# Feed-forward activations of layer 1 quantised inside the attention, its gate and up weights put in place there

## The reference

```python
x = x + _L1_xattn_ref(_layernorm(x), ctx, Wq_d, W_qk, Wkv_d, Wv_u)      # 16 heads, latent keys and values
x = x + _L1_ffn_ref(_layernorm(x), w_gate, w_up, w_down, s_gate, s_up, s_down)

def _L1_ffn_ref(x, ...):            # H = 512, I = 1376
    xq = int4_quant(x)              # beta = mean |x| of the row; clip(round(x * sqrt7 / (beta + eps)), -8, 7)
    gate = bitlinear(xq, w_gate, s_gate)     # w_q = clip(round(w / (mean |w| + eps)), -1, 1), times mean |w|
    up = bitlinear(xq, w_up, s_up)
    inter = int8_quant(up * square(relu(gate)))   # gamma = max |.| of the row; round(x * 127 / gamma)
    return bitlinear(inter, w_down, s_down)
```

## Time and profile before

| | us |
|---|---|
| median of 3 runs | 850.58 (850.53 to 852.6) |
| the profiled execution | 852.77 |
| its span | 851.1 |
| attention of layer 1, last unit's copy ends | 177.02 |
| its last VectorE operation ends | 181.09 |
| first gate matmul | 188.85 |
| last down matmul of the feed-forward part ends | 229.61 |
| first operation of layer 2 | 230.0 |

### The profile page before, as it was taken

One profiled execution on the slowest core, in us unless ns is written; L12 is line 12 of the kernel. 1 busy time (PEld: TensorE's weight loads), 2 busy tenths in 40 slices (PEclk: granted clock), 3 DMA queues, 4 the chain that ended last, 5 costly groups with the idle time before them and its releaser, 6 DMA issues. The chain is left out here.

```text
span 851.1 us, 16359 instructions
## 1 busy us (share of the span) xinstructions
PE 778.3 (91%) x5144; PEld 634.7 (75%) x5150; DVE 700.9 (82%) x1762; ACT 532.3 (63%) x1441; POOL 408.9 (48%) x374
## 2 busy tenths in 40 slices
PE   1995899858988999999999999999999999899988
PEld 0484666534677898898888988989989888776556
DVE  7897988969787887897897897798888888797855
ACT  6865798846457557557657657665665576772541
POOL 3237088805035845844846746745755663401120
PEclk9998999979999999999999999999999999999879
DMA  8245246444120310320320320320310210004001
GB/s 299 108 144 180 77 151 240 145 133 142 29 72 21 106 50 1 99 74 0 99 74 0 99 74 0 99 73 1 99 49 25 75 50 26 1 2 120 1 1 50
DMA packets 37488, 65.67 MB, mean 77 GB/s; under 512 B 5377, under 2 KB 17729, under 8 KB 37314
## 3 DMA queue, kind: packets, MB, share of 16 engines
q1 hardware_dynamic: 37442, 65.10, 23.3%
HBM read 59.76 MB, written 5.33 MB: 76 GB/s over the span
## 5 line engine op out<-in xcount | busy, mean ns | idle before, releaser
L2433 DVE TENSOR_SCALAR_CACHE_REDUCE xn<-ctxT,candidate 128x512 bf16<-128x512 f32 x240 | 168.8, 741 | 0.0
L2080 ACT ACTIVATE layer_attention_probs<-xnT,stats 128x512 f32<-128x512 f32 x128 | 94.0, 734 | 119.2 <-DVE stats L2222 119.2
L1818 PE MATMUL bank<-layer_attention_keysT,layer_attention_queriesT 128*128 128x512 f32 x384 | 120.5, 422 | 5.1 <-DVE layer_attention_queriesT L2215 5.0
L2234 DVE TENSOR_TENSOR layer_attention_probsT<-bank,layer_attention_probsT 128x512 fp32r<-128x512 f32 x128 | 88.1, 688 | 41.2 <-ACT layer_attention_probsT L2088 39.8
L1818 PEld LDWEIGHTS bank<-layer_attention_probsT,layer_attention_values 128*128 128x128 f32 x768 | 98.2, 188 | 11.9 <-DVE layer_attention_probsT L2234 4.2
L2088 ACT CAST layer_attention_probsT<-bank 128x512 fp32r<-128x512 f32 x128 | 74.8, 585 | 50.5 <-PE bank L1901 50.4
L1818 PE MATMUL bank<-layer_attention_probsT,layer_attention_values 128*128 128x256 f32 x768 | 101.5, 281 | 3.3 <-DVE layer_attention_probsT L2234 2.7
L1818 PE MATMUL bank<-layer_attention_l_wkv,layer_context_parts 128*128 128x256 f32 x720 | 93.7, 283 | 0.0
L1818 PE MATMUL bank<-layer_attention_l_wq,layer_attention_xnT 128*128 128x512 f32 x384 | 93.6, 392 | 0.0
L1818 PEld LDWEIGHTS bank<-layer_attention_l_wkv,layer_context_parts 128*128 128x128 f32 x720 | 91.3, 191 | 2.7
L1818 PE MATMUL bank<-layer_attention_wo,layer_attention_headsT 128*128 128x512 f32 x336 | 88.7, 405 | 0.4 <-ACT layer_attention_squares L2039 0.4
(11 more groups left out here) (347 smaller groups left out, 1673.2 us busy)
## 6 DMA issues: line engine op xcount, KB each, us to landing
layer_attention_l_raw_qo<-in_wqT SPq DMA_DIRECT2D x8, 1024.0 KB, 5.5
layer_attention_l_raw_qo<-in_woT SPq DMA_DIRECT2D x8, 1024.0 KB, 6.4
xnT<-inverse_sums SPq DMA_DIRECT2D x14, 512.0 KB, 3.8
tw_raw<-in_w_gateT SPq DMA_DIRECT2D x8, 688.0 KB, 5.2
tw_raw<-in_w_upT SPq DMA_DIRECT2D x8, 688.0 KB, 4.2
tw_raw<-in_w_downT SPq DMA_DIRECT2D x6, 768.0 KB, 4.6
layer_attention_l_raw_kv<-in_wkvT SPq DMA_DIRECT2D x8, 512.0 KB, 5.0
ternary<-tw_rounded SPq DMA_DIRECT2D x8, 344.0 KB, 2.5
```

Of the source, the lines that this page charges most:

```text
L1818: last = pe.matmul(out, stationary[f][a], moving[f][b], start=f == 0 and x == 0, stop=f == count - 1 and x == 2)
L2080: a.activation(probs[:, u % 3, :], masked[:, u % 2, :], ACT.Exp, bias=negmax[:, u:u + 1], scale=-1.0, accum_out=sums[:, u:u + 1]).then_inc ...
L2234: v.tensor_tensor(probsT[:, 1, p % 2, :, columns], T[u % 2][:, :].rearrange("p (c q) -> p c q", c=CPB), probsT[:, 0, p % 2, :, columns], A ...
L2433: own(k.nc.vector.tensor_scalar((k.flags if flags is None else flags)[:, r % 2], row_tile(k.ctxT, r), k.candidate[:, r:r + 1].bitcast(F32) ...
```

## The change

Tiles 0 and 1 are quantised and turned at the end of the attention block instead of at the start of the feed-forward block. Their codes, the up weights and half of the turned codes lie where batch 0's queries were, the gate weights in `xnT` and, with the passes of the quantising, where batch 0's values were. The pieces are rounded in the order gate, down, up; up pieces are written in place and not stored, gate weights are loaded back behind pieces 10, 11 and 12. The feed-forward block starts with the matmuls; the last tile's attention result is added to `x` there, and tiles 2 and 3 are quantised between the first tile's chunks. The update of the bisection moves from u = 55 to u = 62, two counts from the start to the end of the feed-forward block. The chunk after a tile's row maximum comes ahead of its scaling. GpSimd's splits wait for the 8-bit codes of tiles 0 and 1.

```diff
+    ROUNDED = (0, 1, 2, 3, 8, 9, 10, 11, 12, 4, 5, 6, 7)
+    STORED = 9
...
+        if i == tw.STORED:
+            g.wait_ge(scores_psum, TPB * HEADS1)
+        rounded = tw.rounded[0:rows, n % 2, 0:width] if i < tw.STORED else k.front.up[:, f, :]
...
+    for i, piece in enumerate(tw.ROUNDED):
+        if 2 <= i < tw.STORED + 2:
             store(i - 2)
+        elif i >= 2:
+            sp.wait_ge(tw.rounded_ready, i - 1)
+        ternary_load(k, piece, count + i)
+        if i == tw.STORED + 1:
+            for p in range(2):
+                sp.wait_ge(tw.stored[p], 16 * (KT // 2))
+            sp.wait_ge(latent_psum, B)
+            gate_load(0, k.front.gate[0])
+        if i == tw.STORED + 2:
+            gate_load(1, k.front.gate[1])
+        if i == tw.STORED + 3:
+            sp.wait_ge(quads_done, TPB * HEADS1 // 4)
+            gate_load(2, k.front.gate[2])
...
+def front_magnitudes_scalar(k, n, t):
...
+    a.activation(r.x4[:, t, :], k.xn[:, t, :], ACT.Abs, accum_out=r.beta[:, t:t + 1]).then_inc(r.beta_ready, 1)
...
                 turn_mixed(TILES - 1)
+                for t in range(TPB):
+                    front_turn_tensor(k, t)
...
+                    if u == UNITS - 1:
+                        v.wait_ge(S_["probs_ready"], UNITS)
+                        own(v.reciprocal(k.front.inverse[:, :], sums[:, TILES - 1, :]))
                     if u % 4 == 3:
                         copy_turned(u)
...
-                        if counts == 4:
-                            bisection_update(k, own)
+                    if u == UNITS - 2:
+                        bisection_update(k, own)
...
-                divide_mixed(TILES - 1)
-                add_mixed(TILES - 1)
-                v.wait_ge(S_["x_updated"], TILES)
+                front_rounded_vector(k, own, 0)
+                front_codes_vector(k, own, 0)
+                v.wait_ge(S_["mixed_psum"], TILES)
+                v.wait_ge(S_["x_updated"], TILES - 1)
...
+                    if u == 60:
+                        front_magnitudes_scalar(k, following, 0)
...
+                front_magnitudes_scalar(k, following, 1)
+                front_magnitudes_scalar(k, following, 2)
                 copy_mixed(TILES - 1)
...
-                for c, (c0, c1) in enumerate(CHUNKS):
-                    for w in (GATE, UP):
-                        sp.dma_start(wgu[:, w, :, c0:c1], tw.scratch[w].rearrange("(f p) c -> p f c", p=P)[:, :, c0:c1])\
...
+                        if i == 1:
+                            front_magnitudes_scalar(k, n, TILES - 1)
+                        if (t, c) == (2, 0):
+                            x8T_copy(0)
+                    if t == 1:
                         x4T_copy(2)
                         x4T_copy(3)
-                    if t >= 1:
+                    if t >= 2:
                         x8T_copy(t - 1)
...
-                quantise4(0)
-                tile_rows_vector(k, n, TILES - 1)
-                quantise4(1)
...
-                bisection_count(k, own, 0, first_flags(k))
-                for c in range(NC):
-                    inner_chunk(0, c)
-                    if c == 0:
-                        bisection_count(k, own, 1, first_flags(k))
+                scales(0)
+                attention_update()
+                tile_variance_vector(k, TILES - 1)
+                inner_chunk(0, 0)
+                tile_rows_vector(k, n, TILES - 1)
+                inner_chunk(0, 1)
+                front_rounded_vector(k, own, 1)
+                inner_chunk(0, 2)
+                front_codes_vector(k, own, 1)
+                scales(1)
                 for t in range(TILES):
                     magnitude(t)
+                    if t + 1 < TILES:
+                        inner_chunk(t + 1, 0)
                     scaled(t)
                     if t + 1 < TILES:
-                        inner_chunk(t + 1, 0)
+                        inner_chunk(t + 1, 1)
                     own.wait()
                     rounded(t)
-                    if t + 1 < TILES:
-                        inner_chunk(t + 1, 1)
...
                     tile_rows_vector(k, following, t)
+                for j in range(FRONT_COUNTS):
+                    bisection_count(k, own, j, first_flags(k))
...
+                    if t == 0:
+                        pe.wait_ge(x4T_ready, TILES)
...
-                gate_up(0)
-                turn4(2)
-                turn4(3)
-                gate_up(1)
+                pe.wait_ge(tw.gate_loaded, 16 * NC)
+                pe.wait_ge(tw.rounded_ready, len(tw.PIECES))
+                gate_up(0, range(NC))
+                gate_up(1, range(NC))
+                for t in range(TPB, TILES):
+                    pe.wait_ge(x4T_ready, t - 1)
+                    front_turn_tensor(k, t)
+                gate_up(2, range(1))
                 turn8(0)
-                gate_up(2)
+                gate_up(2, range(1, NC))
                 down(0)
                 turn8(1)
-                gate_up(3)
+                gate_up(3, range(NC))
...
+    g.wait_ge(codes_ready, 1)
     g.wait_ge(gw.kv_loaded, 16)
...
+    g.wait_ge(codes_ready, 2)
     g.wait_ge(gw.q_loaded, 16)
```

205 lines of the change are left out of this document (114 added, 91 removed).

## The result

The changed kernel takes 844.41 us in the median (841.79 to 850.39, 10 runs), beside 851.89 of the kernel before (848.17 to 854.68, 10 runs), 7.5 us less. The ratio on record is 0.9927, 95% interval 0.9908 to 0.9947: 6.2 us off (interval 4.5 to 7.8, being 0.0073, 0.0053 and 0.0092 of 851.89). The quotient of the two medians is 0.9912; 0.9927 is what 844.41 gives over 850.58, the median of the first three runs, from which the forecast was made: 7.2 us off, 843.4. The profiled execution of the changed kernel took 842.14 us, its span is 840.4.

A forecast was written before the change was run, and what follows sets the result against it. TensorE, busy 91% of the span, was taken to bound the kernel, with gains only where it waits, chiefly for VectorE's chain. 1.3 + 6.5 - 0.6 = 7.2 us off 850.58 gives 843.4 us, range 841.0 to 848.0.

The forecast's parts named there:

- the stretch: From VectorE's last attention copy to its first layer 2 operation; forecast gain 6.5 us, less 0.6 for the clock.
- Update and magnitudes: Late attention units: moving the update to u = 62 gains 1.3 us; three magnitude passes on ScalarE cost nil.
- Rounding: GpSimd's reordered rounding ends at 169.0 instead of 168.14, tile 0's `rstd` at 169.6; 1.3 us in hand, cost nil.
- Start of the block: Feed-forward start: TensorE begins at about 181.9 instead of 188.85, tile 0's row maximum at 191.0 instead of 197.13.
- Clock: First gate matmuls: a possible fall to half clock after TensorE's short pause, priced at 0.6 us lost.
- Rival A: Clock stays at half through the first two feed-forward chunks: gain 5.6 us, 845.0 us; chance 0.18.
- Tail: Feed-forward end: last norm plus two counts let VectorE end at 223.1, 0.5 us behind TensorE; 6.5 us gained.
- GpSimd's splits: Key, value and query weight splits beside VectorE's scaling and rounding in the feed-forward block: cost nil.
- rival B: Splits block VectorE's scaling or rounding for up to a split operation: gain 5.2 us, 845.4 us; chance 0.14.
- Rival D: Slower: each microsecond of rounding after 170.3 costs one; ending after 180 gives 853.5 us; chance 0.03.
- Rival C: Gate loads slow the piece loads, rounding ends up to 6 us late: 848.1 us at worst; chance 0.10.
- E: The feed-forward block's start is tied to something else, such as the down weights: 850.6 us; chance 0.03.

The follow-up runs named there:

- chunk_first: The kernel before with one edit: the next tile's first chunk product ahead of the scaling. Ratio to the kernel before 1.0023 (0.9995 to 1.0051).
- update_only: The kernel before with only the bisection's update moved, to u = 62 in place of u = 55. Ratio to the kernel before 0.9987 (0.9967 to 1.0006).
- rounding_later: The changed kernel with three more GpSimd passes over the last up piece's raw weights. Ratio to the kernel before 1.0007 (0.9977 to 1.0036).
- splits_free: The changed kernel without GpSimd's two waits for the 8-bit codes ahead of its splits. Ratio to the kernel before 0.9981 (0.9947 to 1.0015).
- before_busy: The kernel before with 18 useless matmuls ahead of the codes' first transposes and 8 ahead of the first gate matmul. Ratio 1.0022 (0.9991 to 1.0053).
- gate_late_busy: The changed kernel with gate transfers only at the feed-forward block's start and 20 useless matmuls in TensorE's wait. Ratio to the kernel before 0.9977 (0.9950 to 1.0004).

## Why the prediction was right, step by step

**The sum.** 1.3 for the update and 5.9 for the stretch (6.5 less 0.6). The traces give 1.86 and 6.06, 7.9 in all; the medians of ten runs 7.5 and the ratio 6.2, with 7.2 inside its interval. The mechanism held in the main, an early front whose two halves are both needed. Part of the close number is luck, as the terms show.

**Update and magnitudes.** The 1.86 us are three terms, not one. The update's move by itself is 1.26 us (chunk_first's 11.51 less update_only's 10.25), as the sum had it. The execution traced of the kernel before adds 1.09 (12.60 less 11.51), most of it with the clock's fall at 170, which the sum didn't have. The magnitudes, put at nil since "the first falls into a wait of ScalarE", cost 0.49. The last two are errors of opposite sign, and the 1.09 aren't there in every execution.

**Rounding.** It ended at 167.39. This execution was 1.42 us ahead already at unit 55 (163.00 against 164.42), so that is 168.8 beside the expected 169.0. The first of GpSimd's three `rstd`, tile 0's, was there at 167.9, 0.55 us behind the rounding, and the norm at 169.38 found it. The margin was 1.5 us (1.3 expected), and rounding_later shows what lay behind it.

**Start of the block.** Counted from the last copy, which the prediction put at 177.2: first gate matmul 4.6 to 4.8 us behind it (expected 4.7), row maximum of tile 0 13.5 (expected 13.8), of tile 3 36.3 (expected 35.8). These terms held.

**Clock.** The 0.6 us were not spent: full clock throughout. TensorE's last down matmul ended 45.1 us behind the copy, and without the 0.6 the prediction had 45.4. I priced the clock only as a small loss of the change, but more hangs on it: with TensorE idle for 4.57 us ahead of the gate matmuls the same block loses 2.15 us more than the lateness. Rival A did not come about there. Further on, behind the idle 2.17 us before the third chunk of tile 1, the clock falls in some executions, and costs 1.1 to 1.2 us, less than A's 1.6. So the trace's 6.06 us for the stretch are those of an execution without that fall.

**Tail.** Predicted 0.5 us of VectorE behind TensorE, measured 1.22. Counted from the copy, TensorE ended 0.3 us sooner than expected and VectorE 0.5 later (46.4 against 45.9). What made VectorE late: the scaling (1.34) and rounding (1.28) of tile 2 lie beside the queries' split and take 0.41 us each over their 0.93 and 0.87.

**GpSimd's splits.** Nil, but for those 0.8 us, is right for the kernel as written and wrong as a view of the machine. The prediction said of rival B that the rows "show less than a third of that". They showed little because few operations met. splits_free shows operations that wait for a whole instruction of GpSimd, one for each small one on 128x2 numbers. The two waits for the 8-bit codes are thus worth 5.9 us of the stretch, the clock's part included. Rival B named the mechanism; the change avoids it.

**Rival D** had each microsecond of rounding beyond 170.3 cost one. In rounding_later, 2.74 us of waiting cost 6.85 us at layer 2. At this one point the slope is over 2 (in single executions, but the ratio says the same), so by an estimate from it D's point of decision lay several microseconds nearer than 180. I took it for remote with too much ease. Rival C (a late rounding) did not come about, nor did E.

**What stays open.** From layer 2's first operation to the end the fourteen profiled executions take 619.7 us (changed) to 625.4 us (before_busy) for the same work; the kernel before takes 621.05. The three kernels with halves undone are 1.6 to 2.7 us ahead of the kernel before at layer 2, and their ratio is 1.000. The clock has a hand in such spreads: in 100 executions of the kernel before, in the four groups, the 15 with a mean granted clock of 0.98 or more took 848.8 us in the mean, the 22 with 0.972 or less 853.5. But it isn't all. After layer 2's first operation the traces have between 11 and 24 us of half clock, and chunk_first, with the least, is among the longest there (625.1 us). So how much of the step from 7.9 us in two traces to 7.5 or 6.2 in the times is the clock stays open.

## What to carry to other kernels

Price a wait on the path by what it does to TensorE's clock too: here 2.7 us of waiting cost 6.9, and undoing either half of an early start lost nearly all that the two gained together. Before a difference of about 1 us between two traces is put down to an edit, compare a stretch that the edit doesn't reach: here two such stretches moved by 1.0 to 1.2 us with the clock. Before two-input or SBUF-to-SBUF work of VectorE is laid beside GpSimd, count the meetings: a small operation can cost a whole instruction of GpSimd, so a wait that keeps GpSimd back may be the best edit of a change. What an operation of VectorE costs in a row tells only of the meetings that happened in that trace.

## What the runs showed of the hardware

An operation of VectorE on 128x2 numbers lasts 0.2 us alone and 1.2 to 1.9 beside GpSimd's splits, where one on 128x1 keeps its 0.2 (splits_free); the time stands in its own length, not as idle, so nothing in the list of waits points to it. In gate_late_busy matmuls of no use began 1.15 us behind other work and the clock stayed at 1.00. In before_busy they began 2.11 us behind it and came too late: the granted clock fell to 0.50 at 179.2, 0.9 us ahead of them, and 18 of them then took 6.95 us instead of 3.8. An idle 2.17 us at the same place of two nearly equal kernels was followed by 1.2 GHz in one and 2.4 in the other, and so was an idle 1.48 us in two programs that are alike up to there.
